# A tuned attention and expert kernel: the opening in two halves of two batches, x loaded chunk by chunk, input layouts by partition, value weights folded earlier

## The chip, the cores and the metric

The kernel runs on one core of one Trainium2 chip. The metric is the time of one execution on the device in microseconds (us). Three runs of the kernel before gave 667.72, 667.65 and 667.26 us, so the median is 667.65 us.

## The reference

x has 32 batches of 128 tokens of 128 features, the context 32 batches of 128 tokens of 64 features. Everything is f32.

```
x = x + tanh(g_xattn) * attention(layernorm(x), ctx)    # 16 heads of 64
        q = ln(x) @ Wq ; k = ctx @ Wk ; v = ctx @ Wv
        softmax(q k^T / 8) v, then @ Wo + bo
x = x + tanh(g_ffn) * experts(layernorm(x))             # 32 experts of 64, and a shared one of 128
        sigmoid router, 2 of 4 groups, then 8 experts; weights normalised, times 2.5
        sum over experts of w_e * down_e(silu(gate_e(x)) * up_e(x)), plus the shared expert
```

## The kernel before

The 32 batches are eight chunks of four. An attention stage runs over all chunks (chunk 0 unrolled, chunks 1 to 6 in a hardware loop, chunk 7 unrolled), then an expert stage over all chunks. Every engine has an instruction list of its own, written out by hand; the engines meet only in semaphores, and within an engine nothing overtakes. SyncE (SP) issues all DMAs, all of them in one queue.

Scores are not computed from q and k. A = Wq Wk^T is folded per head (`fold`, line 1255), and G = ln(x) A is projected per pair of batches (`g_project`, line 1161, into PSUM banks 0 to 3). Scores are then G times the context. In the same way C = Wv Wo replaces values and output projection. The block-diagonal tiles `wk_diag` and `wv_diag` are filled with zeros by GpSimd (POOL), lines 444 and 445, and SP loads the weights into them after that (`load_diag`, line 319). Products of f32 quality are made of three fp32r products of high and low parts: ScalarE (ACT) writes the high part (`xt_high`, `g_high`, `a_high`), VectorE (DVE) subtracts for the low part (`xt_low`, `g_low`, `a_low`).

For each batch t the row maxima are taken first: PE computes scores once (`max_scores`, line 1176), DVE reduces them (`take_max`, line 788), PE transposes the maxima (`transpose_max`, line 1193), ACT copies them out (`max_out`, line 540), and SP moves them by DMA into the tile `max_rows` (`load_max_row`, line 289), from where they enter the transposed scores (`scores`, line 1199) as a product with minus one. ACT takes the exponential, PE weighs the context (`weigh`, line 1219), and ACT copies the result out (`u_out`). The row sums go by DMA to another layout (`spread_sums`, line 297), DVE inverts them (`invert`, line 796), the inverse goes out to DRAM and back (lines 304 to 317), and DVE normalises (line 802).

The opening (the prologue) is what stands ahead of the loop on each engine:

- SP loads x of chunk 0, Wq, Wk, a context tile, Wv, Wo, small inputs, more context tiles, then x of chunks 1 to 7 in one DMA (line 344), two slices of the expert weights (`w_raw`), and then waits to send the row maxima of batch 0 (line 348).
- PE runs five products to keep itself busy (`keep_busy`), folds A in two halves, transposes ln(x) of four batches, projects G of batches 0 and 1 and of 2 and 3, takes the first scores of batches 0 and 1, and folds C last (lines 1282 to 1285).
- DVE computes the layer norm of chunk 0 (stats, 12 levels of small operations for the inverse root, and `apply` on four batches), then the low parts, then maxima of batch 0, the low parts of the second G, maxima of batch 1, and the stats of chunk 1 (`chunk_stats`, line 698).
- ACT writes the high parts, and computes tanh of the gates (line 584) once they and the bias have come in.

In chunk 0 of attention SP's order for batch b is: row maxima of b+1, sums of b-1, context and expert weights to come, inverse of b-1. On DVE chunk 0 holds extra work that later chunks don't have: the stats of chunks 2 to 7 (`STATS_AT`, line 70: chunks 2, 3, 4, 5 at steps 2, 3, 4, 5 and chunks 6 and 7 at step 6, where a step is half a batch), and the inverse roots for them. `invert` of the batch before stands ahead of the stats in the second half of a batch, and the low parts of the next G stand behind both.

```
            if h == 1:                                   # DVE, batch b, second half
                invert(t - 1, ...)
            ...
                chunk_stats(n)                           # first chunk only
            if h == 1 and b % 2 == 1 and not last:
                g_low(...)                               # scores of batch t + 1 wait for this
```

Of the kernel before, what the change touches and what calls it, by code (L numbers as in the profile page):

```python
# [31 lines left out]
P = 128  # L32
NB = 32
# [36 lines left out]
STATS_AT = {2: (2,), 3: (3,), 4: (4,), 5: (5,), 6: (6, 7)}  # L70
NB_SEAM = (NCH - 2) * CB
# [5 lines left out]
def build(nc, x, ctx_nat, ctx_t, g_xattn, g_ffn, wq_t, wk_t, wv_t, wo, bo, router_t, router_bias, experts, out):  # L77
    with ExitStack() as stack:
# [97 lines left out]
        fold_ps = (bank[0], bank[2])  # L176
        early_ps = ((bank[6:8], bank[4:6]), (bank[0:2], bank[4:6]))
# [3 lines left out]
        x_in = [sem("x_in0"), sem("x_in1")]  # L181
# [13 lines left out]
        xt_done, xhi_ready, xlo_ready = sem("xt_done"), sem("xhi_ready"), sem("xlo_ready")  # L195
        g_done, ghi_ready, glo_ready = sem("g_done"), sem("ghi_ready"), sem("glo_ready")
# [31 lines left out]
        x_dram = x.rearrange("b n d -> n b d")  # L228
        out_dram = out.rearrange("b n d -> n b d")
# [43 lines left out]
        def _(sp):  # L273
# [70 lines left out]
            sp.dma_start(x_sb[:, CB:NB, :], x_dram[:, CB:NB, :]).then_inc(x_in[1], 16)  # L344
            for slot in range(2):
                load_weights(slot, slot * WSTEP)
            sp.wait_ge(const_ready, 1)
            load_max_row(0, 0, -2)

            def attention(c, first, last):  # L350
                for b in range(CB):
                    t = CB * c + b
                    if not (last and b == CB - 1):
                        load_max_row(t + 1, (b + 1) % 2, t - 1)
                    if not (first and b == 0):
                        spread_sums(t - 1, (b - 1) % 2)
# [47 lines left out]
            def store_result(c):  # L404

                wait_first(result_ready, c + 1)
                sp.dma_start(out_dram[:, bass.ds(c * CB, CB), :], result.rearrange("p (b d) -> p b d", b=CB))\
                    .then_inc(result_free, 16)
# [34 lines left out]
        def _(pool):  # L443
# [64 lines left out]
            pool.wait_ge(x_in[1], 16)  # L508
# [16 lines left out]
        def _(act):  # L525
            def xt_high(i):
# [3 lines left out]
                nc.scalar.activation(xnt_hi[:], ut_ps[:], ACT.Copy).then_inc(xhi_ready, 1)  # L530

# [49 lines left out]
            xt_high(0)  # L581
            a_high(1)
            act.wait_ge(small_in, 16 * 3)
# [3 lines left out]
            g_high(0, 0)  # L587
# [101 lines left out]
        def _(dve):  # L689
# [8 lines left out]
            def chunk_stats(n):  # L698

                for b in range(CB):  # L700
                    nc.vector.bn_stats(bn6[:, 0, b, :], tile_of(CB * n + b)).then_inc(ln_step[0], 1)
                wait_first(ln_step[0], 2 * CB * n + CB)
                for b in range(CB):
                    nc.vector.bn_aggr(mean_var[:, 0, CB * n + b, :], bn6[:, 0, b, :]).then_inc(ln_step[0], 1)
                dve.wait_ge(ln_step[0], 2 * CB * (n + 1))

# [50 lines left out]
            def apply(which, t):  # L757

                for b in range(CB):
# [16 lines left out]
            def xt_low(i):  # L776
                dve.wait_ge(xhi_ready, i + 1)
                nc.vector.tensor_tensor(xnt_lo[:], ut_ps[:], raw(xnt_hi[:]), ALU.subtract).then_inc(xlo_ready, 1)

# [189 lines left out]
            dve.wait_ge(x_in[0], 16)  # L969
# [3 lines left out]
            ln_apply(0, 0)  # L973
# [8 lines left out]
            xt_low(0)  # L982
            a_low(1)
            g_low(0, 0)
# [3 lines left out]
            g_low(1, 1)  # L988
            for h in range(2):
# [3 lines left out]
            dve.wait_ge(x_in[1], 16)  # L993
            dve.wait_ge(const_ready, 6)
            chunk_stats(1)
# [151 lines left out]
        def _(pe):  # L1147
# [13 lines left out]
            def g_project(ring, chunk, bank_free):  # L1161

                pe.wait_ge(xlo_ready, chunk + 1)
                for j in range(4):
                    s, value = bank_free[j // 2]
                    wait(pe, s, value + j % 2)
# [281 lines left out]
```

## Time and profile before

| | |
|---|---|
| median of three runs | 667.65 us |
| profiled execution, its own time | 665.77 us |
| span of its trace | 664.0 us |
| PE busy | 650.2 us, 98% |
| DVE busy | 499.3 us, 75% |
| ACT busy | 365.4 us, 55% |
| POOL busy | 284.2 us, 43% |
| DMA queue q1 (all of SP's transfers) | 65.07 MB, 39.9% of 16 engines |
| TensorE clock granted | 1.00 of full |

PE is TensorE's matmul, PEld its weight load, SPq the issue of a DMA on SP. A number in brackets in a timeline is idle time of the engine ahead of the instruction, with what ended it. "issue" in the chain of waits is time in which the engine waited for nothing that the profile shows. A landing time is counted from the start of the issue to the data's arrival.

### The profile page before, as it was taken

Reading aid. Unit: us, or ns where it says so; the run is one execution under the profiler, and the core shown is the slowest. Engines: PE = TensorE matmul, PEld = TensorE weight load, DVE = VectorE, ACT = ScalarE, POOL = GpSimd, SP = SyncE. Lnnn points to the kernel's source line nnn. Section 1 sums busy time; section 2 is a strip of 40 time slices with the busy share of each in tenths; the row PEclk is TensorE's granted clock in tenths of the full one; section 3 lists DMA queues with packets and bytes.
Section 4 is the critical chain, followed back from the end, with each engine's and each line's share of the span. In section 5 each row is a group of like instructions: output and inputs, shape, how many; then the busy total and the mean of one; then the engine's idle time right before and its main releaser. Section 6 shows DMA issues by size and latency. Waiting matters only on the chain.

```text
span 664.0 us, 13629 instructions
## 1 busy us (share of the span) xinstructions
PE 650.2 (98%) x3668; PEld 472.1 (71%) x3668; DVE 499.3 (75%) x1331; ACT 365.4 (55%) x690; POOL 284.2 (43%) x316
## 2 busy tenths in 40 slices
PE   8999999999999999999999999999999999999997
PEld 5656666666667676676658778788887878888785
DVE  6989857777586775867787979968696877869565
ACT  3564556565465654655556455565655555555553
POOL 4222323233131332324202656656565656656553
PEclk9999999999999999999999999999999999999999
DMA  7323323232322323223225735273644536364650
GB/s 186 98 64 82 92 65 79 62 84 63 83 75 68 90 63 80 64 78 94 52 67 138 174 89 131 74 182 85 156 119 111 130 72 156 85 159 112 133 141 16
DMA packets 63276, 65.58 MB, mean 99 GB/s; under 512 B 26112, under 2 KB 41600, under 8 KB 63232
## 3 DMA queue, kind: packets, MB, share of 16 engines
q1 hardware_dynamic: 63232, 65.07, 39.9%
q8 instruction: 18, 0.29, 0.2%
q14 instruction: 26, 0.21, 0.1%
HBM read 61.64 MB, written 2.88 MB: 97 GB/s over the span
## 4 chain that ended last, share of the span: by engine, by line
PE 68%; issue 8%; POOL 8%; DVE 6%; DMA 5%; SPq 3%; ACT 1%; POOLq 0%; DVEq 0%; ACTq 0%
PE bank L1151 12%; PE bank L1227 12%; PE bank L1152 11%; PE bank L1153 11%; POOL halves L516 7%; PE bank L1251 6%; PE bank L1187 4%; PE bank L1207 2%; PE bank L1216 2%; PE bank L1210 2%; PE bank L1213 2%; DVE area L806 2%; DMA inverse_dram<-inverse 1%; DMA inverse_bc<-inverse_dram 1%; SPq L294 1%
## 5 line engine op out<-in xcount | busy, mean ns | idle before, releaser
L516 POOL TENSOR_TENSOR halves<-area,halves 128x512 fp32r<-128x512 f32 x134 | 174.0, 1299 | 141.0 <-ACT halves L650 136.5
L663 ACT ACTIVATE area<-bank 128x512 f32<-128x512 f32 x136 | 81.4, 598 | 109.3 <-PE bank L1153 106.7
L602 ACT ACTIVATE area<-bank 128x512 f32<-128x512 f32 x128 | 69.5, 595 | 117.3 <-PE bank L1216 117.3
L1107 DVE TENSOR_TENSOR bank<-area,bank 128x512 f32<-128x512 f32 x128 | 88.6, 692 | 51.1 <-PE bank L1153 50.8
L1227 PE MATMUL bank<-area,ctx_keys 128*65 128x512 f32 (+1 forms) x256 | 124.6, 599 | 0.2 <-ACT u_odd L550 0.2
L1151 PE MATMUL bank<-x2t_hi,w_hi 128*128 128x512 f32 x272 | 110.3, 405 | 1.4 <-DVE area L1118 1.3
L1152 PE MATMUL bank<-x2t_hi,w_lo 128*128 128x512 f32 x272 | 107.1, 394 | 0.0
L1153 PE MATMUL bank<-x2t_lo,w_hi 128*128 128x512 f32 x272 | 106.3, 391 | 0.0
L462 POOL TENSOR_TENSOR ctx_hi<-ctx_raw,ones_col 128x128 fp32r<-128x128 f32 x32 | 18.8, 588 | 197.3 <-DMA ctx_raw<-ctx_t 197.3
L792 DVE TENSOR_REDUCE row_max<-bank 128x4 f32<-128x512 f32 x128 | 81.7, 680 | 25.4 <-PE bank L1187 21.0
L650 ACT ACTIVATE halves<-area 128x512 fp32r<-128x512 f32 x136 | 85.1, 626 | 21.1 <-DVE area L1118 20.7
L1118 DVE TENSOR_TENSOR area<-bank,wbc 128x512 f32<-128x512 f32 x128 | 86.3, 679 | 1.5 <-DMA wbc<-rows_dram 1.5
L806 DVE TENSOR_TENSOR area<-u_odd,inverse_bc 64x1024 f32<-64x1024 f32 x32 | 39.9, 1248 | 42.7 <-DMA inverse_bc<-inverse_dram 42.2
L1251 PEld LDWEIGHTS bank<-c_pair,area 128*128 128x128 f32 x512 | 61.3, 192 | 11.2 <-issue 8.6
L1227 PEld LDWEIGHTS bank<-area,ctx_keys 128*65 128x65 f32 (+1 forms) x256 | 37.1, 164 | 39.3 <-issue 38.6
L1251 PE MATMUL bank<-c_pair,area 128*128 128x128 f32 x512 | 62.5, 275 | 0.0
L1151 PEld LDWEIGHTS bank<-x2t_hi,w_hi 128*128 128x128 f32 x272 | 51.1, 188 | 14.2 <-DVE area L1118 3.9
L1153 PEld LDWEIGHTS bank<-x2t_lo,w_hi 128*128 128x128 f32 x272 | 51.1, 188 | 12.0
L1152 PEld LDWEIGHTS bank<-x2t_hi,w_lo 128*128 128x128 f32 x272 | 51.2, 188 | 10.2
L1151 PE MATMUL bank<-halves,w_hi 128*128 128x512 f32 x136 | 54.3, 399 | 0.5 <-POOL halves L516 0.5
L1187 PEld LDWEIGHTS bank<-ctx_hi,halves 64*128 64x128 f32 x512 | 33.4, 186 | 30.1 <-issue 23.9
L1153 PE MATMUL bank<-halves,w_hi 128*128 128x512 f32 x136 | 53.9, 396 | 0.0
(129 smaller groups left out, 1087.7 us busy)
## 6 DMA issues: line engine op xcount, KB each, us to landing
wbc<-rows_dram SPq DMA_DIRECT2D x126, 256.0 KB, 4.4
inverse_bc<-inverse_dram SPq DMA_DIRECT2D x64, 256.0 KB, 3.9
w_raw<-experts SPq DMA_DIRECT2D x32, 102.0 KB, 2.0
ctx_raw<-ctx_t SPq DMA_DIRECT2D x32, 64.0 KB, 1.9
ctx_keys<-ctx_nat SPq DMA_DIRECT2D x32, 64.0 KB, 2.1
out<-area SPq DMA_DIRECT2D x7, 256.0 KB, 4.1
max_rows<-max_t SPq DMA_DIRECT2D x64, 4.0 KB
area<-wq_t SPq DMA_DIRECT2D x1, 512.0 KB, 4.4
```

Of the source, the lines that this page charges most:

```text
L516: nc.gpsimd.tensor_tensor(hid_lo[:, u % SLOTS, :], hid[:, u % HIDS, :], raw(hid_hi[:, u % SLOTS, :]), ALU.subtract).then_inc(hidlo_ready, 1)
L602: nc.scalar.activation(probs_t[:, k, :, :], st_ps[q][:].rearrange("p (h n) -> p h n", h=4), ACT.Exp)\
L650: nc.scalar.activation(hid_hi[:, u % SLOTS, :], hid[:, u % HIDS, :], ACT.Copy).then_inc(hidhi_ready, 1)
L663: nc.scalar.activation(silu_g[:, u % 2, :], gate_ps[u % 2][:], ACT.Silu).then_inc(silu_ready, 1)
L792: nc.vector.tensor_reduce(row_max[:, parity, first:first + 4], ps[q][:].rearrange("p (h m) -> p h m", h=4), AX_X, ALU.max)\
L1107: nc.vector.tensor_tensor(up_ps[u % UPS][:], silu_g[:, u % 2, :], up_ps[u % UPS][:], ALU.mult)\
L1118: nc.vector.tensor_tensor(hid[:, u % HIDS, :], up_ps[u % UPS][:], wbc[:, group % WBC_SLOTS, i, :], ALU.mult).then_inc(hid_ready, 1)
L1151: nc.tensor.matmul(ps, wh, xh, start=start, stop=False)
L1152: nc.tensor.matmul(ps, wl, xh, start=False, stop=False)
L1153: return nc.tensor.matmul(ps, wh, xl, start=False, stop=stop)
L1227: nc.tensor.matmul(u_ps[q][0:CD + 1 if q == 0 else P, :], keys, probs_t[:, k, :, :].rearrange("p i n -> p (i n)"), start=True, stop=True). ...
L1251: ins = nc.tensor.matmul(ps, u_t[:, parity, p, :], c_pair[:, p, :], start=p == 0, stop=p == PAIRS - 1)
```

## The change

- x, Wq, Wo and the output are laid out by partition: one partition's part of a transfer is one contiguous piece (2 KB for a chunk of x, 4 KB for Wq and Wo), where it was pieces of 512 B. The transposes of inputs and output are outside the kernel.
- x is loaded chunk by chunk: chunk 1 where chunks 1 to 7 stood, then the row maxima of batch 0, then the two slices of expert weights and chunk 2. Chunks 3 and 4 are issued in batch 0, chunks 5 and 6 in batch 1, chunk 7 in batch 2, each time behind the row maxima and ahead of the sums.
- Wk is loaded as soon as its own tile is zeroed.
- In the opening the norm's `apply`, the transposes and the high and low parts of ln(x) go in two halves of two batches. G of batches 0 and 1 needs the first half alone.
- On ACT tanh of the gates moves behind the high parts of the first G.
- C is folded ahead of the first scores of batch 1, where it was behind them.
- DVE takes the first step of chunk 1's stats ahead of the maxima of batch 1.

```diff
+X_AT = {0: (3, 4), 1: (5, 6), 2: (7,)}
+        xt_ps = bank[6:8]
-        x_in = [sem("x_in0"), sem("x_in1")]
+        x_in = [sem(f"x_in{n}") for n in range(NCH)]
 # SP
-            sp.dma_start(x_sb[:, 0:CB, :], x_dram[:, 0:CB, :]).then_inc(x_in[0], 16)
-            sp.dma_start(wq_pair, wq_t.rearrange("(p r) n -> r p n", r=P)).then_inc(wqk_in, 16)
-            sp.wait_ge(zeroed, 2)
+            def load_x(n):
+                tiles = slice(CB * n, CB * n + CB)
+                sp.dma_start(x_sb[:, tiles, :], x[:, tiles, :]).then_inc(x_in[n], 16)
+            load_x(0)
+            sp.dma_start(wq_pair, wq_t).then_inc(wqk_in, 16)
+            sp.wait_ge(zeroed, 1)
             for q in range(2):
                 load_diag(wk_diag, wk_t, q, wqk_in)
             load_raw(0, 0)
+            sp.wait_ge(zeroed, 2)
             for q in range(2):
                 load_diag(wv_diag, wv_t, q, wvo_in)
-            sp.dma_start(wo_pair, wo.rearrange("(p r) n -> r p n", r=P)).then_inc(wvo_in, 16)
+            sp.dma_start(wo_pair, wo).then_inc(wvo_in, 16)
...
-            sp.dma_start(x_sb[:, CB:NB, :], x_dram[:, CB:NB, :]).then_inc(x_in[1], 16)
+            load_x(1)
+            sp.wait_ge(const_ready, 1)
+            load_max_row(0, 0, -2)
             for slot in range(2):
                 load_weights(slot, slot * WSTEP)
-            sp.wait_ge(const_ready, 1)
-            load_max_row(0, 0, -2)
+            load_x(2)
 
             def attention(c, first, last):
                 for b in range(CB):
                     t = CB * c + b
                     if not (last and b == CB - 1):
                         load_max_row(t + 1, (b + 1) % 2, t - 1)
+                    if first:
+                        for n in X_AT.get(b, ()):
+                            load_x(n)
                     if not (first and b == 0):
                         spread_sums(t - 1, (b - 1) % 2)
...
-                sp.dma_start(out_dram[:, b:b + CB // 2, :],
+                sp.dma_start(out[:, b:b + CB // 2, :],
 # POOL
-            pool.wait_ge(x_in[1], 16)
 # ACT
+            def xt_high_half(half):
+                act.wait_ge((xt_begun, xt_done)[half], 1)
+                nc.scalar.activation(xnt_hi[:, halved(half)], xt_ps[half][:, halved(half)], ACT.Copy)\
+                    .then_inc((xhi_begun, xhi_ready)[half], 1)
             a_high(0)
-            xt_high(0)
+            xt_high_half(0)
             a_high(1)
+            g_high(0, 0, range(2))
+            xt_high_half(1)
+            g_high(0, 0, range(2, 4))
             act.wait_ge(small_in, 16 * 3)
             nc.scalar.activation(tanh_g[:], gates[:], ACT.Tanh).then_inc(tanh_ready, 1)
...
-            g_high(0, 0)
             g_high(1, 1, range(3))
 # DVE (chunk_stats is cut in chunk_stats_begin, which waits for x_in[n], and chunk_stats_end)
-            ln_apply(0, 0)
+            dve.wait_ge(rstd_step[0], RSTD_STEPS)
+            apply(0, 0, range(2))
             a_low(0)
-            xt_low(0)
+            xt_low_half(0)
+            apply(0, 0, range(2, 4))
             a_low(1)
-            g_low(0, 0)
+            g_low(0, 0, range(2))
+            xt_low_half(1)
+            g_low(0, 0, range(2, 4))
             (maxima of batch 0)
             g_low(1, 1)
+            chunk_stats_begin(1)
             (maxima of batch 1)
             dve.wait_ge(router_in, 32)
-            dve.wait_ge(x_in[1], 16)
             dve.wait_ge(const_ready, 6)
-            chunk_stats(1)
+            chunk_stats_end(1)
 # PE
             fold(wq_pair, wk_diag, 0, fold_ps[0])
             pe.wait_ge(const_ready, 6)
-            transpose_norm(0, ut_ps)
+            transpose_half(0)
             fold(wq_pair, wk_diag, 1, fold_ps[1])
-            g_project(0, 0, ((glo_ready, -2), (glo_ready, -2)))
+            g_project(0, 0, None, range(2))
+            transpose_half(1)
+            g_project(0, 0, None, range(2, 4))
+            pe.wait_ge(xlo_ready, 1)
             max_scores(0, 0, 0, 0, early_ps[0][0])
             max_scores(0, 0, 0, 1, early_ps[0][1])
             g_project(1, 0, ((glo_ready, 1), (glo_ready, 3)))
             transpose_max(0, 0)
+            pe.wait_ge(wvo_in, 16 * 3)
+            fold(wv_diag, wo_pair, 0, early_ps[0][0][0])
             pe.wait_ge(maxt_ready, 1)
+            fold(wv_diag, wo_pair, 1, early_ps[0][0][1])
             pe.wait_ge(glo_ready, 4 + 2)
             max_scores(1, 1, 0, 0, early_ps[1][0])
             max_scores(1, 1, 0, 1, early_ps[1][1])
-            pe.wait_ge(wvo_in, 16 * 3)
-            pe.wait_ge(max_ready, 2)
-            for i in range(2):
-                fold(wv_diag, wo_pair, i, early_ps[0][0][i])
```

## Rows read from the trace of the kernel before

**Rows 1.** The page: busy times, and PE's granted clock in 40 slices.
```profile
PE 650.2 (98%) x3668; PEld 472.1 (71%) x3668; DVE 499.3 (75%) x1331; ACT 365.4 (55%) x690; POOL 284.2 (43%) x316
...
PEclk9999999999999999999999999999999999999999
```

**Rows 2.** The chain of waits, 18 to 26 us: start us, us, what.
```profile
19.19 0.41 issue
...
25.28 0.83 issue
```

**Rows 3.** The chain of waits, 40 to 61 us.
```profile
40.41 0.28 issue
...
42.97 0.14 ACT max_t L543
...
45.39 1.85 DMA sums<-u_odd
...
60.82 0.50 PE bank L1207 x2
```

**Rows 4.** PE and weight loads in time order, opening: start us, us [idle before].
```profile
6.58 0.19 PEld L1264 LDWEIGHTS bank<-c_pair 128*128 128x128 f32 x1 [0.24 <-issue]
7.26 1.04 PEld L1258 LDWEIGHTS bank<-area 128*128 128x128 f32 x8 [0.49 <-DMA area<-wk_t]
...
11.28 0.38 PE L1151 MATMUL bank<-xnt_hi,a_hi 128*128 128x256 f32 x1 [0.52 <-DVE xnt_lo L778]
...
19.60 1.11 PE L1187 MATMUL bank<-ctx_hi,halves 64*128 64x128 f32 x16 [0.72 <-ACT max_t L543]
```

**Rows 5.** ACT in time order, opening.
```profile
12.27 0.20 ACT L584 ACTIVATE tanh_g<-gates 128x2 f32<-128x2 f32 x1 [0.88 <-DMA bo_bc<-bo]
```

**Rows 6.** DVE in time order, opening and first chunk.
```profile
10.53 0.69 DVE L778 TENSOR_TENSOR xnt_lo<-bank,xnt_hi 128x512 fp32r<-128x512 f32 x1 [0.68 <-ACT xnt_hi L530]
...
13.43 2.48 DVE L783 TENSOR_TENSOR halves<-bank,halves 128x512 fp32r<-128x512 f32 x4 [1.31 <-ACT halves L536]
...
20.61 2.47 DVE L792 TENSOR_REDUCE row_max<-bank 128x4 f32<-128x512 f32 x4
23.00 0.86 DVE L701 BATCH_NORM_STATS2 bn<-x_sb 128x6 f32<-128x128 f32 x4
24.02 0.38 DVE L704 BATCH_NORM_AGGREGATE mean_var<-bn 128x2 f32<-128x6 f32 x4 [0.15 <-DVE bn L701]
24.72 1.29 DVE L792 TENSOR_REDUCE row_max<-bank 128x4 f32<-128x512 f32 x2 [0.33 <-DVE mean_var L704]
...
36.56 0.25 DVE L800 RECIPROCAL inverse<-sums 128x16 f32<-128x16 f32 x1 [0.34 <-DMA sums<-area]
...
38.10 2.48 DVE L783 TENSOR_TENSOR halves<-bank,halves 128x512 fp32r<-128x512 f32 x4
```

**Rows 7.** SP's issues in time order.
```profile
27.61 0.38 SPq L280 DMA_DIRECT2D ctx_keys<-ctx_nat  x1
32.61 1.33 SPq L294 DMA_DIRECT2D max_rows<-max_t  x2
34.06 1.20 SPq L302 DMA_DIRECT2D sums<-area  x2
```

**Rows 8.** One line's instructions: SP's issue time in ns, min/median/max.
```profile
L287 SPq DMA_DIRECT2D w_raw<-experts x6: 351/356/4572, 13.2 to 55.3; - x6
L407 SPq DMA_DIRECT2D out<-area x7: 524/524/1510, 414.2 to 639.1; - x7
```

**Rows 9.** DMA issues of the page: count, KB each, median us to landing.
```profile
out<-area SPq DMA_DIRECT2D x7, 256.0 KB, 4.1
...
x_sb<-x SPq DMA_DIRECT2D x1, 256.0 KB, 2.9
...
out<-area SPq DMA_DIRECT2D x2, 128.0 KB, 1.9
...
gates<-g_xattn SPq DMA_DIRECT2D x1, 0.5 KB, 4.1
```

More of the change, by code:

```diff
@@ L225, in wait @@
             eng.wait_ge(s, value)
-        x_dram = x.rearrange("b n d -> n b d")
-        out_dram = out.rearrange("b n d -> n b d")
         def pairs_of(h):
@@ L406, in store_result @@
                 wait_first(result_ready, c + 1)
-                sp.dma_start(out_dram[:, bass.ds(c * CB, CB), :], result.rearrange("p (b d) -> p b d", b=CB))\
+                sp.dma_start(out[:, bass.ds(c * CB, CB), :], result.rearrange("p (b d) -> p b d", b=CB))\
                     .then_inc(result_free, 16)
@@ L705, in chunk_stats @@
                 dve.wait_ge(ln_step[0], 2 * CB * (n + 1))
+            def chunk_stats(n):
+                chunk_stats_begin(n)
+                chunk_stats_end(n)
             def batch_stats(t, b):
@@ L755, in rstd_level, with apply @@
                     ins.then_inc(stepped, 1)
-            def apply(which, t):
-                for b in range(CB):
+            def apply(which, t, batches=range(CB)):
+                for b in batches:
                     nc.vector.tensor_scalar(xn[:, b, :], tile_of(t + b),
@@ L778, in xt_low, with xt_low_half @@
                 nc.vector.tensor_tensor(xnt_lo[:], ut_ps[:], raw(xnt_hi[:]), ALU.subtract).then_inc(xlo_ready, 1)
+            def xt_low_half(half):
+                dve.wait_ge((xhi_begun, xhi_ready)[half], 1)
+                nc.vector.tensor_tensor(xnt_lo[:, halved(half)], xt_ps[half][:, halved(half)], raw(xnt_hi[:, halved(half)]),
+                                        ALU.subtract).then_inc((xlo_begun, xlo_ready)[half], 1)
             def g_low(g, ring, banks=range(4)):
@@ L1159, in transpose_norm, with transpose_half, g_project @@
                 ins.then_inc(xt_done, 1)
[L1161 to L1166, printed above, removed]
+            def transpose_half(half):
+                pe.wait_ge(xn_ready, 2 * half + 2)
+                for i in range(2 * half, 2 * half + 2):
+                    ins = nc.tensor.transpose(xt_ps[half][:, i * P:(i + 1) * P], xn[:, i, :], ident[:])
+                ins.then_inc((xt_begun, xt_done)[half], 1)
+            def g_project(ring, chunk, bank_free, banks=range(4)):
+                if bank_free is None:
+                    pe.wait_ge(xlo_begun, 1)
+                else:
+                    pe.wait_ge(xlo_ready, chunk + 1)
+                for j in banks:
+                    if bank_free is not None:
+                        s, value = bank_free[j // 2]
+                        wait(pe, s, value + j % 2)
                     if j % 2 == 0:
@@ L1423, with by_pair @@
     ctx = np.asarray(ctx_512)
+    def by_pair(w):
+        return lay(np.asarray(w).reshape(PAIRS, P, D).transpose(1, 0, 2))
     def up(w, shared):
@@ L1443 @@
     ins = [nc.dram_tensor(n, a.shape, F32, kind="ExternalInput").ap() for n, a in arrays.items()]
-    out = nc.dram_tensor("out", (NB, P, D), F32, kind="ExternalOutput").ap()
+    out = nc.dram_tensor("out", (P, NB, D), F32, kind="ExternalOutput").ap()
     build(nc, *ins, out)
     r = run_bass_kernel_spmd(nc, [arrays], core_ids=[0])
-    return r.results[0]["out"]
+    return lay(np.asarray(r.results[0]["out"]).transpose(1, 0, 2))
```

12 lines of the change are left out of this document (7 added, 5 removed).

## The prediction

> **What bounds the kernel now.** I read the page first: PE is busy for 650.2 of 664.0 us at full granted clock [rows 1]. So a change in the opening can give back no more than PE's own gaps there, and whatever moves the first chunk moves everything behind it, one for one, as long as PE stays the engine that the rest waits for. The chain of waits comes next, since it shows where PE is not the bound. In the opening it leaves PE twice: 0.41 us at 19.2 and 0.83 us at 25.3 [rows 2]. PE's own timeline has the first of these as 0.72 us of idle time ahead of the first scores of batch 1, ended by ACT's copy of the maxima [rows 4]. From 26.1 to 40.4 PE has no idle time. Then comes a third stretch [rows 3], and it is the one that decides this case: PE waits 0.28 us at 40.41, the chain goes over ACT's `max_out` (42.97) to SP, which issues the maxima and then the sums of batch 1, the sums land at 47.24 after 1.85 us, DVE inverts them at once, and from there DVE's list of chunk 0 (normalise, stats, maxima, low parts) ends just ahead of PE's scores at 60.82. So between 40 and 61 us the end is set by an SP queue, a small DMA and a full DVE, not by PE. DVE's own timeline shows the same thing one batch earlier: the inverse of batch 0 at 36.56 was preceded by 0.34 us of waiting for the sums, and behind it stand the stats and the four `g_low` from 38.10 to 40.58, which end just ahead of PE's scores at 40.69 [rows 6].
>
> **The opening, step by step.** PE's fold of A begins at 7.26, after 0.49 us in which its weight load waited for Wk [rows 4]. The weight load before it had a gap of 0.24 us, which is the warm-up's own pace, so 0.25 us can go at most when Wk comes sooner (SP waits for one memset instead of two). I take 0.25; bounds 0 and 0.25. Then the halves. Before, DVE needs `apply` on four batches, then the low part of A, and waits 0.68 us for ACT's high part, and `xt_low` takes 0.69; PE starts G at 11.28 [rows 4 to 6]. Now `apply` on two batches is ready at about 8.3, PE transposes two batches at 8.3 to 8.6, ACT writes the high part of A 8.3 to 8.9 and half of x 8.9 to 9.25 (half of the 0.68), DVE does `a_low` to 9.65 and half of `xt_low` (0.35) to 10.0. G starts at 10.05, 1.2 us sooner. ACT is no longer held by tanh, which waited for a DMA until 12.27 [rows 5]; high parts of G start at about 11.1. With six products a bank at 0.12 us, the two transposes between, and one high and one low part of about 0.6 us each behind bank 3, the four `g_low` end at 14.8 where they ended at 15.91 (13.43 + 2.48) [rows 6]: 1.1 us sooner.
>
> From there DVE is full in both versions: four maxima (2.47), four `g_low` (2.48), and now one `bn_stats` group (0.86) ahead of the maxima of batch 1 instead of behind them. That puts these maxima at 20.65 to 23.15 where they ended at 23.08, and the first scores of batch 2 on PE must wait for them. PE has meanwhile folded C in the gap of 0.72 us, but it gains nothing by it: it ends the scores of batch 0's first half near 22.6 and waits for DVE at 23.2. The `bn_aggr` (0.38) and the start-up of 0.33 seen ahead of 24.72 [rows 6] bring the maxima of batch 2 to 23.95, against 24.72. **Gain of the opening: 0.77 us**, bounds 0.4 (if the half-size instructions cost what whole ones do: about 0.35 more in all) and 1.66 (both gaps, 0.72 + 0.83, and 0.1 of change, if DVE turned out not to hold PE). I take 0.77 since it is the sum of DVE's rows.
>
> **The x loads inside batches 0 to 2.** Chunks 3 and 4 go behind the maxima of batch 1, where SP has time: it issues nothing from 28.0 to 32.6 [rows 7], so their cost is nothing; without that gap it would be two issues. Chunks 5 and 6 are otherwise. SP is held until ACT copies out the maxima of batch 2 (issue at 32.61, now 31.84 with the 0.77), issues them for 1.33 us, and then directly the sums at 34.06 [rows 7]. Two loads now stand between. No row of before issues such a load in a quiet queue; the nearest are 0.35 us (102 KB) and 0.52 us (256 KB, out) [rows 8]. I take 0.45 and 0.05 between two issues, so 1.0 us, bounds 0.8 and 1.15. The sums are issued 1.0 - 0.77 = 0.23 us later than before. The second load is in the queue as well: a load of 256 KB takes 2.9 us to land [rows 9], the second sum DMA is issued 1.15 us after it and needs 1.85, so the load lands at the very time the sums would; I add 0.1. The inverse of batch 0, which waited for these sums even before, comes 0.3 us later than 36.56, and with it `g_low`, and with that PE's scores at 40.69: **the whole gain of the opening is gone, and 0.3 us more** (bounds -0.3 and +0.75). The cost of SP's two issues is paid whole because what DVE has saved is spent waiting.
>
> Chunk 7 goes behind the maxima of batch 3, again directly ahead of the sums, and this is the chain of [rows 3] itself: SP's maxima, sums, 1.85 us, DVE. Nothing hides it. **0.45 + 0.05 = +0.5 us** (bounds 0.4 and 0.57). Its data are through the rings before the sums' (1.1 us between their issues, as above). DVE is full from there to 60.7, so it carries to PE at 60.82. PE had 0.82 us of slack ahead of `g_low` at 59.8, so it takes no part.
>
> **What stays.** The stats of chunks 2 to 7 find their x in time: chunk 7 is issued near 45 and lands near 48, its stats are at 52. Chunk 1's stats no longer wait (x lands at about 15). The one transfer of chunks 1 to 7 blocked SP's issue of `w_raw` for up to 4.57 us [rows 8], but SP then waited for ACT's maxima anyway, so that gain is 0. The end: two stores of 128 KB land in 1.9 us after issue [rows 9], which is also what 4 KB of sums take, so their bytes cost hardly anything; 0 to 0.1 for larger pieces, I take 0.05.
>
> The Trainium skill's page "DMA: Bandwidth & Descriptors" (Specifications) has 512 B as the smallest piece for full rate. By that rule the new layout gives nothing, as pieces were 512 B already; if instead the first x and Wk landed 0.3 us sooner, the fold would still wait for the warm-up, so the sum is the same but for the 0.25 above. No row of before holds a load of 2 KB pieces of x.
>
> **The sum.** +0.3 + 0.5 - 0.05 = +0.75 us. The profiled execution took 665.77 us around a span of 664.0, the median is 1.88 us above the former: I predict 666.5 for such an execution with a span of 664.7, and 667.65 + 0.75 = **668.4 us** for the median. That is 0.11%: a measurement of this kernel tells about 0.2% (1.3 us) from no change, so the forecast is "no change", a shade slower.
>
> **Rivals.**
>
> A. *The loads are hidden, the opening's gain survives.* If SP issued the x loads in idle time, or the sums were not late, -0.77 - 0.05: 666.8 us. For it: 0.34 us of waiting at 36.56 is short [rows 6], and an issue may be cheaper than I take. Against: SP's order puts the loads between two DMAs that follow one another directly [rows 7]. Chance 0.23.
>
> B. *Slower: the sums queue behind x.* Place: the same two points. From 3.0 us on for the landing of chunk 6 (1.15 + 1.85) each further tenth is added to the inverse. A 0.5 KB DMA of the gates, issued behind 512 KB of Wo, took 4.1 us to land [rows 9]. If x5 and x6 land like the 256 KB stores (4.1 us), the sums of batch 0 are 37.9 against 36.5, +1.35, and chunk 7 adds 48.85 - 47.24 = +1.6: 670.6 us; half of it gives 669.5. Against: the first x took 2.9. Chance 0.17. The same page, in "Queues, rings and completion order", says that each DMA engine consumes its ring in order and that a semaphore's increment lands only after all earlier writes of that engine; by this rule B's queueing is real, and only the bytes ahead decide its size. The trace agrees in the gates' 4.1 us.
>
> C. *Faster by more than the bound.* Both gaps of PE vanish (0.72 + 0.83 and 0.1, as above), and neither load costs anything: -1.65, 666.0 us. For it: PE's list has the work to fill the first gap. Against: DVE is full from 13.4 to 24.4 [rows 6], and PE can't pass it. Chance 0.18, more than the rows give, since a gain in one of the many small moves may be missing in my sum.
>
> **How the numbers follow.** The forecast (between +0.1 and +1.3) has 0.42, A with all between -1.3 and +0.1 has 0.23, B 0.17, C 0.18. C and most of B lie beyond 0.2%. Faster 0.18, same 0.65, slower 0.17. The range leaves out half of C and the far part of B: 666.2 to 669.6 us. The forecast's own bounds are -0.3 + 0.4 - 0.1 = 0.0 and 0.75 + 0.57 = +1.3: 667.65 to 669.0.
>
> **What would show it.** In the changed kernel's trace: G starts near 10.05; the maxima of batch 1 end near 23.2 and PE waits for them with 0.5 us or more; the first maxima of batch 2 near 23.95; SP issues chunk 5 near 33.2 and the sums near 34.3; DVE's inverse of batch 0 near 36.9 with over 1 us of waiting for sums; PE's scores of batch 2 near 41.0 with about 1 us of idle ahead; the inverse of batch 1 near 48.05; PE's scores of batch 4 near 61.6 (60.82 + 0.8). If these scores come ahead of 60.8, the step that fails is the price of SP's issues; if they are right and the time is not, something behind 61 us has moved, which I hold to be carried over unchanged.

## The result, and the profile after

The changed kernel is slower. On the first chip it took 670.15 us (median of 8, 668.93 to 671.58) against 667.92 us for the kernel before (8 runs): ratio 1.0036, interval 1.0025 to 1.0048, or about +2.4 us (the medians differ by 2.2). A second chip gave 667.58 against 665.13 us (12 and 24 runs), ratio 1.0034, interval 1.0023 to 1.0044. The prediction was 668.4 us, or +0.75 us, "no change", with a range of 666.2 to 669.6. The profiled execution took 671.03 us around a span of 669.2. That is 5.2 us over the one of before, more than the medians differ, so below each reading is set against a second profile of each kernel.

The start first. TensorE's weight loads in the changed kernel (columns: start us, us, engine, line and operation; in brackets the idle time before and what ended it):

```profile
5.90 0.34 PEld L1310 LDWEIGHTS bank<-c_pair 128*128 128x128 f32 x1 [0.52 <-issue]
7.33 0.19 PEld L1310 LDWEIGHTS bank<-c_pair 128*128 128x128 f32 x1 [0.24 <-issue]
8.19 0.19 PEld L1304 LDWEIGHTS bank<-area 128*128 128x128 f32 x1 [0.24 <-DMA area<-wk_t]
```

In the warm-up a load takes 0.34 us until 7.3 us and 0.19 from there: the step from half to full speed, though the column of the granted clock says 1.00 throughout. The fold of A starts at 8.19, where it started at 7.26 [rows 4]. Wk is issued sooner than before (1.72 us against 2.61), but it is not there sooner: it lands at 8.02 here, against 7.22 in the kernel before.

The opening behind it, in VectorE's and TensorE's timelines:

```profile
20.79 0.86 DVE L719 BATCH_NORM_STATS2 bn<-x_sb 128x6 f32<-128x128 f32 x4
21.64 2.48 DVE L824 TENSOR_REDUCE row_max<-bank 128x4 f32<-128x512 f32 x4
25.10 1.29 DVE L824 TENSOR_REDUCE row_max<-bank 128x4 f32<-128x512 f32 x2 [0.69 <-DVE mean_var L725]
24.38 0.66 PE L1233 MATMUL bank<-ctx_hi,halves 64*128 64x128 f32 x8 [0.75 <-DVE row_max L824]
```

VectorE runs full and TensorE waits for its maxima (0.75 us), as forecast. From the first weight load of the fold to the maxima of batch 2 it is 16.91 us (25.10 - 8.19), against 17.46 (24.72 - 7.26) in [rows 4, 6].

SyncE's queue around the sums of batch 0 and of batch 1, against [rows 7]:

```profile
32.99 1.34 SPq L295 DMA_DIRECT2D max_rows<-max_t  x2
34.37 0.91 SPq L326 DMA_DIRECT2D x_sb<-x  x2
35.40 1.20 SPq L303 DMA_DIRECT2D sums<-area  x2
45.20 1.41 SPq L295 DMA_DIRECT2D max_rows<-max_t  x2
46.65 0.43 SPq L326 DMA_DIRECT2D x_sb<-x  x1
47.20 1.19 SPq L303 DMA_DIRECT2D sums<-u_odd  x2
```

And the inverses and scores that wait for those sums, against [rows 3, 6]:

```profile
38.49 0.25 DVE L832 RECIPROCAL inverse<-sums 128x16 f32<-128x16 f32 x1 [1.33 <-DMA sums<-area]
50.06 0.25 DVE L832 RECIPROCAL inverse<-sums 128x16 f32<-128x16 f32 x1 [1.24 <-DMA sums<-u_odd]
42.61 0.50 PE L1253 MATMUL bank<-halves,ctx_hi 64*128 64x512 f32 x2 [0.54 <-issue]
63.57 0.50 PE L1253 MATMUL bank<-halves,ctx_hi 64*128 64x512 f32 x2 [0.32 <-DVE halves L815]
```

The sums of batch 0 are issued 2.41 us behind the beginning of the maxima's issue (before 1.45), and VectorE idles 1.33 us for them (before 0.34). The scores of batch 4 are 2.75 us late. Behind that the distance still grows, by different amounts: this profile is 4.9 us behind that of before at the last inverse, and the two second profiles, 2.06 us apart at S4 below, are 3.0 us apart there. No run isolates this part.

Three marks cut the start into pieces that can be compared over all twelve profiles. F is the fold's first weight load, I0 and I1 are the inverses of batch 0 and 1, S4 the first scores of batch 4, in us from the span's start:

| profile | F | I0 - F | I1 - I0 | S4 |
|---|---|---|---|---|
| before | 7.26 | 29.30 | 10.70 | 60.82 |
| before, second | 7.46 | 29.12 | 10.70 | 60.99 |
| E4 layouts alone | 7.60 | 29.09 | 10.70 | 60.90 |
| changed | 8.19 | 30.30 | 11.57 | 63.57 |
| changed, second | 7.79 | 30.23 | 11.51 | 63.05 |
| E9 x5, x6 in one DMA | 7.79 | 29.63 | 11.56 | 62.49 |
| E5 three small issues | 8.19 | 30.34 | 11.25 | 63.29 |
| E1 x all in batch 0 | 8.47 | 28.73 | 11.07 | 61.78 |
| E8 x behind the sums | 7.81 | 28.59 | 11.39 | 61.30 |
| E6 stats 1 in batch 0 | 7.78 | 30.09 | 11.38 | 62.96 |
| E7 warm-up 4 | 7.44 | 29.75 | 11.09 | 61.79 |
| E10 stats 1 in the gap | 7.44 | 28.55 | 11.06 | 60.55 |

The changed kernel loses in each column: 0.3 to 0.9 us at F, 1.0 to 1.1 in I0 - F, 0.8 to 0.9 in I1 - I0. F is not a perfect mark. Where Wk sets it (E8 and E9), the maxima of batch 2 are issued 24.5 us behind it; where the warm-up sets it (both profiles of the changed kernel, E1, E5) it is 24.8. So differences of 0.3 us in I0 - F between these two kinds say nothing.

For the landing one more table is needed. Each row is the second of a pair of sums DMAs, with what was issued directly ahead of the pair; times in us from the span's start.

| profile, batch | directly ahead | it lands at | sums issued | sums land |
|---|---|---|---|---|
| before, batch 0 | nothing | - | 34.66 | 36.54 |
| E1, batch 0 | nothing | - | 35.31 | 37.17 |
| changed, batch 0 | x5, x6 | 38.11 | 36.00 | 38.47 |
| changed, second, batch 0 | x5, x6 | 37.65 | 35.59 | 37.99 |
| E9, batch 0 | x5 and x6 in one | 36.99 | 34.79 | 37.40 |
| E5, batch 0 | two of 0.5 KB | 38.15 | 35.99 | 38.50 |
| changed, batch 1 | x7 | 49.70 | 47.78 | 50.04 |
| E5, batch 1 | one of 0.5 KB | 49.32 | 47.85 | 49.76 |

With nothing ahead the sums land 1.86 to 1.88 us after their issue. With a DMA ahead they land 0.34 to 0.44 us behind it, unless their own 1.86 us end later: in the last row 47.85 + 1.86 is 49.71, so there the DMA ahead costs next to nothing. In these rows the sums are never complete before what stood ahead of them, and the price is set by when that lands.

### The profile page after: what moved, and what is told of

It is laid out like the page before. It is cut to its first block, busy times and chain, and to the rows that moved or that the text cites. A ratio compares the mean times of both kernels' runs of the same rounds, so it can differ in the third digit from the quotient of the medians.

```text
span 669.2 us, 13635 instructions
## 1 busy us (share of the span) xinstructions
PE 652.6 (98%) x3668; PEld 472.5 (71%) x3668; DVE 500.8 (75%) x1332; ACT 365.7 (55%) x691; POOL 286.0 (43%) x316
## 3 DMA queue, kind: packets, MB, share of 16 engines
HBM read 61.64 MB, written 2.88 MB: 96 GB/s over the span
## 4 chain that ended last, share of the span: by engine, by line
PE 53%; issue 11%; DMA 9%; POOL 8%; DVE 7%; SPq 6%; ACT 2%; DVEq 1%; POOLq 0%; ACTq 0%
PE bank L1186 11%; PE bank L1187 10%; PE bank L1188 10%; POOL halves L525 7%; PE bank L1273 7%; DMA inverse_bc<-inverse_dram 4%; PE bank L1297 3%; PE bank L1233 3%; SPq L295 2%; DMA inverse_dram<-inverse 2%; DVE area L838 2%; PE bank L1253 2%; DVE halves L815 2%; DVE row_max L824 2%; DMA sums<-area 1%
## 5 line engine op out<-in xcount | busy, mean ns | idle before, releaser
L472 POOL TENSOR_TENSOR ctx_hi<-ctx_raw,ones_col 128x128 fp32r<-128x128 f32 x32 | 21.4, 667 | 199.3 <-DMA ctx_raw<-ctx_t 199.3
```

## The experiments

Ratios are to the kernel before on the same chip, with their intervals. E2 and E3 are each half of the change. Line numbers are those of each kernel's own file.

**E1, all remaining x in batch 0.**

```
-X_AT = {0: (3, 4), 1: (5, 6), 2: (7,)}
+X_AT = {0: (3, 4, 5, 6, 7)}
```

> The changed kernel with x chunks 3 to 7 all issued in batch 0, where SP has about 4 us of idle time, and none in batches 1 and 2. Theory 1 (SP's issues of x and the x data ahead of the sums are what costs): in the changed kernel the sums of batch 0 left 0.96 us later behind the maxima and landed after 2.45 instead of 1.85 us, those of batch 1 0.47 us later and after 2.26 instead of 1.85 us; all four go, -2.4 us against the changed kernel, so the time is within 0.2% of before (667.0 to 668.8 us), the sums follow the maxima by 1.45 to 1.55 us, and PE's scores of batch 4 start near 61.2. Theory 2 (the loss comes from the opening and from waits in later chunks, the loads are nearly free): at most -0.8 us, so 669.3 or more.

Measured: 666.40 against 666.26 us, 1.0001 (0.9991 to 1.0011). The five loads are issued in 2.34 us that SyncE has free (E1's queue and VectorE's inverses):

```profile
27.35 2.34 SPq L326 DMA_DIRECT2D x_sb<-x  x5
34.70 1.20 SPq L303 DMA_DIRECT2D sums<-area  x2
37.20 0.25 DVE L832 RECIPROCAL inverse<-sums 128x16 f32<-128x16 f32 x1 [0.33 <-DMA sums<-area]
48.27 0.25 DVE L832 RECIPROCAL inverse<-sums 128x16 f32<-128x16 f32 x1 [0.74 <-DMA sums<-u_odd]
```

The wait for the sums of batch 0 is back at 0.33 us, the loss is gone. The place of three loads is the whole slowdown, as far as an interval of 0.1% to either side can tell; all else together is worth nothing that can be measured.

In batch 1 VectorE still waits 0.74 us (before 0.38), though nothing stands directly ahead of the sums. Their landing is told in 16 steps; 15 have come by 47.93 us and the last at 48.25. While these packets move, from 47.10 to 47.45, one transfer of 8 KB runs in an instruction queue (E1's DMA from 47.0 to 47.5: queue, kind, packets, MB, share of 16 engines):

```profile
q14 instruction: 1, 0.01, 4.3%
```

E2, E6, E7, E8 and E10 have the same late last step, by 0.3 to 0.7 us, each with such a transfer among or just ahead of the packets; the kernel before and E4 have neither. This coincidence was not tested by a run.

**E8, the same loads in the same batches, behind the sums.**

```
+                    if not (first and b == 0):
+                        spread_sums(t - 1, (b - 1) % 2)
                     if first:
                         for n in X_AT.get(b, ()):
                             load_x(n)
-                    if not (first and b == 0):
-                        spread_sums(t - 1, (b - 1) % 2)
```

> The changed kernel with one move: SP issues the sums first and the x loads behind them, in the same batches (x3, x4 in batch 0; x5, x6 in 1; x7 in 2). Same loads, same bytes, same SP time in all. Theory 1 (the cost is that a load stands ahead of the sums, on the path SP, sums, inverse): sums 1.45 us behind the beginning of max_rows in batch 1 and not 2.4, inverse of batch 0 within 0.4 us of the wait-free value, time that of the kernel with all x in batch 0: ratio 1.000 to 1.001 to the kernel before. Theory 2 (any x load near the sums costs, before or behind, since it delays ctx, w_raw and the inverses behind it in the queue): ratio 1.002 to 1.0035, with the idle time at inverse_dram or inverse_bc instead.

Measured: 667.79 against 667.21 us, 1.0010 (0.9999 to 1.0021). In E8's queue:

```profile
33.74 1.20 SPq L303 DMA_DIRECT2D sums<-area  x2
34.98 1.05 SPq L326 DMA_DIRECT2D x_sb<-x  x2
```

and on its VectorE:

```profile
36.40 0.24 DVE L832 RECIPROCAL inverse<-sums 128x16 f32<-128x16 f32 x1
46.24 1.22 DVE L838 TENSOR_TENSOR area<-area,inverse_bc 64x1024 f32<-64x1024 f32 x1 [0.43 <-DMA inverse_bc<-inverse_dram]
```

The sums no longer make VectorE wait at all in batch 0. Theory 1 holds for most of the loss. A part of theory 2 is there as well: the inverse's broadcast is now what comes late (0.43 us, where the changed kernel, E1 and the kernel before have no wait).

**E5, three DMAs of 0.5 KB in place of x5, x6 and x7, on top of E1.**

```
+for n in {1: (0, 1), 2: (2,)}.get(b, ()):
+    sp.dma_start(tiny[:, n:n + 1], g_xattn...broadcast_to([P, 1])).then_inc(tiny_in, 16)
```

> The kernel with all five remaining chunks of x loaded in batch 0 (ratio 1.0001 to the kernel before), plus three DMAs of 0.5 KB that nothing waits for, issued by SP where the changed kernel issues x5, x6 and x7: two between max_rows and sums of batch 1, one between them in batch 2. It has the changed kernel's time on SP's queue, and none of its 256 KB in the rings. Theory 1 (SP's issue time is most of the +2.4 us): sums is issued 2.4 us after max_rows begins in batch 1 (instead of 1.45) and 0.45 later in batch 2, lands in 1.85 us as before, the inverse of batch 0 is 0.9 to 1.0 later than in that kernel and the time +1.4 us, ratio about 1.002. Theory 2 (the transfers of x ahead of sums are the cost): the time is that kernel's, ratio 0.999 to 1.001. Estimate from the changed kernel's trace (0.96 and 0.47 us of issue, 0.6 and 0.4 of landing): +1.4 of the 2.4 stays.

Measured: 668.78 us, 1.0056 (1.0034 to 1.0078), beside 1.0034 for the changed kernel on that chip. E5's queue and inverse:

```profile
34.35 0.91 SPq L368 DMA_DIRECT2D tiny<-g_xattn  x2
35.38 1.21 SPq L305 DMA_DIRECT2D sums<-area  x2
38.53 0.25 DVE L837 RECIPROCAL inverse<-sums 128x16 f32<-128x16 f32 x1 [1.93 <-DMA sums<-area]
```

Theory 1 had the issue right and the landing wrong, and theory 2 fails. 1 KB ahead of the sums costs in I0 - F what 512 KB do (30.34 against 30.30 us): the same 0.91 us of issue, and a landing of the sums of batch 0 in 2.5 us, where the changed kernel has 2.4 to 2.5 and E1, E8 and the kernel before, with nothing directly ahead, have 1.8 to 1.9. The reason is in the table: the second of the small DMAs lands 3.3 us after its issue, as late as x6 (3.3 us). So bytes alone do not set the price. What does is not separated here: each small DMA writes 4 bytes to each of 128 partitions, so it has as many pieces as a load of x, and no run had a DMA of few pieces in this place. E5's higher median has another part: in half of its runs the granted clock is 0.997, and in its profile the expert stage falls back by a further 1.3 us between 400 and 655 us, which no row of the first 64 us explains.

**E9, x5 and x6 as one DMA of 512 KB.**

```
-X_AT = {0: (3, 4), 1: (5, 6), 2: (7,)}
+X_AT = {0: (3, 4), 2: (7,)}
+if b == 1:
+    sp.dma_start(x_sb[:, CB * 5:CB * 7, :], x[:, CB * 5:CB * 7, :]).then_inc(x_pair, 16)
```

> The changed kernel with chunks 5 and 6 of x in one DMA of 512 KB instead of two of 256 KB, in the same place ahead of the sums of batch 1. Theory 1 (what costs is the number of issues, their time on SP and one more DMA in the rings ahead of the sums, and not the bytes): sums issued 0.45 us sooner than in the changed kernel, landing 2.1 us instead of 2.45, time 0.5 to 0.8 us below the changed kernel: ratio 1.002 to 1.003 to before. Theory 2 (bytes in the rings): issue 0.45 us sooner, but the sums land as much later, ratio 1.0034 as for the changed kernel.

Measured: 669.57 us, 1.0041 (1.0028 to 1.0055), 5 runs. In E9:

```profile
33.63 0.44 SPq L365 DMA_DIRECT2D x_sb<-x  x1
34.18 1.20 SPq L304 DMA_DIRECT2D sums<-area  x2
37.42 0.25 DVE L835 RECIPROCAL inverse<-sums 128x16 f32<-128x16 f32 x1 [1.24 <-DMA sums<-area]
```

From the issue of the maxima to the inverse it is 5.17 us, against 5.50 and 5.44 in the changed kernel: one issue less (0.48 us) brings 0.3. The rest goes in the landing, 2.6 and 2.9 us for the two sums DMAs, not shorter, so half of each theory holds. (Of the 0.6 us that I0 - F is shorter, the other 0.3 stands ahead of the queue, from the mark F.) One DMA ahead thus delays the landing no less than two, which a price per DMA would not give. The time does not follow: its interval overlaps the changed kernel's. For the time this run is inconclusive.

**The changed kernel again.**

> The changed kernel again, on the chip of the three others, for a comparison without a change of chip and a second profile. Expected: ratio 1.003 to 1.005; sums 2.4 us behind the beginning of max_rows in batch 1, landing 2.3 to 2.6 us; scores of batch 2 1.3 to 1.9 us later than in the kernel before and of batch 4 2.2 to 2.8. If the landing of sums were 1.85 us here, the rings would not be part of the cause.

Measured: ratio 1.0034, S4 at 63.05, sums issued 2.41 us behind the maxima, landing in 2.4 us in batch 0 and 2.2 in batch 1: as expected.

**The kernel before again.**

> The kernel before again, for a second profile. If the time at which TensorE's clock rises in the warm-up (4.8 us in the first profile, 6.5 to 7.6 in those of the new opening) varies from execution to execution, the fold starts here at 7.3 to 8.6 us; if it belongs to the kernel's order, at 7.3 again. Sums land in 1.85 us in both batches if that is the price without other DMAs ahead.

Measured: 665.98 us, profiled once. Its weight loads:

```profile
5.04 0.34 PEld L1264 LDWEIGHTS bank<-c_pair 128*128 128x128 f32 x1 [0.52 <-issue]
5.74 0.19 PEld L1264 LDWEIGHTS bank<-c_pair 128*128 128x128 f32 x1 [0.37 <-issue]
7.46 0.19 PEld L1258 LDWEIGHTS bank<-area 128*128 128x128 f32 x1 [0.24 <-DMA area<-wk_t]
```

The clock rose at 5.7 us here and at 4.8 in the first profile, with the same instructions on TensorE. Over all profiles the rise lies between 4.8 and 7.6 us, so it varies by execution. Where it is early, Wk sets F (E8 and E9: Wk lands at 7.8 us); where it is late, the warm-up does.

**E7, four warm-up products instead of five, on top of E1** (`-WARM_UP, GAP = 5, 1` / `+WARM_UP, GAP = 4, 1`).

> The kernel with all remaining x in batch 0, and four warm-up matmul groups instead of five. Theory 1 (the fold's start is set by the warm-up, run in the trace at half speed until 7.3 to 8.0 us, and by Wk only if that lands later): fold starts up to 0.86 us sooner, time -0.3 to -0.8 us, ratio 0.9988 to 0.9995. Theory 2 (Wk's landing, at about 7.3 to 7.6 us, sets it): no change, ratio 1.000. Theory 3 (with less warm-up the clock is still low when the fold begins): the fold's own weight loads take 0.34 us instead of 0.19 and the opening is up to 1 us longer, ratio 1.0005 to 1.0015.

Measured: 666.05 us, 1.0014 (0.9999 to 1.0029). F is 7.44 with Wk the last to come, a microsecond sooner than in E1, and then it is lost (E7 by stretch: us, busy time of the engines, granted clock, DMA share, GB/s):

```profile
20.00:24.00 4.00, 2.87 (x34) 2.26 (x32) 3.54 (x12) 1.77 (x3) 1.24 (x3) 1.00 0.41 122
24.00:28.00 4.00, 4.00 (x23) 2.27 (x20) 3.31 (x13) 0.27 (x1) 0.32 (x1) 0.57 0.16 46
```

TensorE was busy for 2.87 of 4 us, and then its granted clock fell to 0.57 as the mean of 4 us, so to the lower level, 1.2 GHz, for most of them. Four other profiles have 2.86 to 2.88 us in the same stretch without a fall (the second of the changed kernel, E6, E8, E9), and only 4 of E7's 12 runs show 0.997 or less over the span. So the fall explains this profile, not the median: the other eight runs have a median of 665.96 us. None of the three theories had this.

**E6, the statistics of chunk 1 moved to batch 0, on top of E1.**

```
-STATS_AT = {2: (2,), 3: (3,), 4: (4,), 5: (5,), 6: (6, 7)}
+STATS_AT = {0: (1,), 2: (2,), 3: (3,), 4: (4,), 5: (5,), 6: (6, 7)}
-            chunk_stats_begin(1)
-            chunk_stats_end(1)
```

> The kernel with all remaining x in batch 0, and the statistics of chunk 1 moved from ahead of the maxima of batch 1 to batch 0 behind the first row of maxima of batch 2. Theory 1 (in the opening VectorE is the engine that runs full from the maxima of batch 1, and what stands on it ahead of the maxima of batch 2 delays them one for one): the 0.86 + 0.38 us of bn_stats and bn_aggr leave, of which 0.5 to 0.9 is gained at the scores that wait for row_max, ratio 0.9985 to 0.999 to the kernel before. Theory 2 (that time is given back behind: the same VectorE work then stands ahead of the inverse of batch 0, and TensorE, which waits for sums, starts batch 2 no sooner): ratio 1.000 to 1.0005.

Measured: 668.79 us, 1.0049 (1.0031 to 1.0067), worse than either theory. E6's VectorE:

```profile
21.23 2.48 DVE L824 TENSOR_REDUCE row_max<-bank 128x4 f32<-128x512 f32 x4 [0.77 <-PE bank L1231]
24.80 1.29 DVE L824 TENSOR_REDUCE row_max<-bank 128x4 f32<-128x512 f32 x2 [1.09 <-PE bank L1231]
```

The room is not used: TensorE folds C (1.95 us) ahead of the scores of batch 1, so VectorE waits for it, and behind it the later maxima and the inverse slip (I0 - F 30.09 against 28.73). So in the opening two engines hold the end at once. The time has a second part, below.

**E10, chunk 1's statistics in VectorE's gap, C folded later.** `load_x(1)` stands right behind Wk, `chunk_stats(1)` right behind the first `apply`, and on TensorE:

```
-            fold(wv_diag, wo_pair, 0, early_ps[0][0][0])
-            pe.wait_ge(maxt_ready, 1)
-            fold(wv_diag, wo_pair, 1, early_ps[0][0][1])
             max_scores(1, 1, 0, 0, early_ps[1][0])
             max_scores(1, 1, 0, 1, early_ps[1][1])
+            fold(wv_diag, wo_pair, 0, early_ps[0][0][0])
+            pe.wait_ge(maxt_ready, 1)
+            fold(wv_diag, wo_pair, 1, early_ps[0][0][1])
```

> A version meant to beat both: the kernel with all remaining x in batch 0, chunk 1 of x loaded right behind Wk, its statistics (0.86 + 0.38 us of VectorE) done in the 1.73 us in which VectorE waits for the high part of A, and the fold of C behind the first scores of batch 1 again, since in the kernel with these statistics in batch 0 TensorE's fold held VectorE's maxima of batch 1 for 0.77 us. Theory 1 (VectorE and the fold of C are together what sets the maxima of batch 2): maxima of batch 2 15.6 us behind the fold's start instead of 16.49, everything to the scores of batch 4 0.7 to 0.9 us sooner, ratio 0.9985 to 0.9992 to before. Theory 2 (the load of x ahead of the context delays the context or Wv, or the fold of C now holds TensorE): ratio 1.000 to 1.001. If TensorE idles more and its granted clock falls, the ratio is above 1.002.

Measured: 668.37 us, 1.0025 (1.0014 to 1.0037). It is the earliest of all at S4 (60.55 us) and yet slower than both E1 and the kernel before. At 410 us, in the first expert chunk, the same instruction of VectorE in E10:

```profile
408.59 0.70 DVE L1141 TENSOR_TENSOR bank<-area,bank 128x512 f32<-128x512 f32 x1 [0.39 <-issue]
410.00 1.23 DVE L776 TENSOR_TENSOR ln_small<-ln_small 128x8 f32<-128x8 f32 x1
414.50 0.51 PE L1185 MATMUL bank<-x2t_hi,w_hi 128*128 128x512 f32 x1 [0.81 <-DVE area L1152]
```

and in E1:

```profile
410.39 0.35 DVE L776 TENSOR_TENSOR ln_small<-ln_small 128x8 f32<-128x8 f32 x1
```

A stall of 0.39 and one of 0.9 us that have no releaser, and TensorE waits 0.81 us for it. E6 has the same two stalls on the same instructions, E1, the changed kernel and the kernel before have not. Against E1's profile everything behind moves by 1.25 us. E6 and E10 are the two kernels in which VectorE's instructions ahead of that point stand in another order than in the changed kernel. That the stall is the fetch of VectorE's code falling elsewhere is a guess, not shown: E1 too has an instruction transfer of 8 KB at this place (410.79 us, in E10 410.17) and no stall. Without the 1.25 us E10 would be at about 667.1 us (668.37 - 1.25), which is the kernel before, not a gain.

**E4, the layouts alone:** the kernel before, x still in two DMAs, with

```
-            sp.dma_start(wq_pair, wq_t.rearrange("(p r) n -> r p n", r=P)).then_inc(wqk_in, 16)
+            sp.dma_start(wq_pair, wq_t).then_inc(wqk_in, 16)
...
-            sp.dma_start(x_sb[:, CB:NB, :], x_dram[:, CB:NB, :]).then_inc(x_in[1], 16)
+            sp.dma_start(x_sb[:, CB:NB, :], x[:, CB:NB, :]).then_inc(x_in[1], 16)
```

and the same for `wo` and `out`.

> The kernel before with the new layouts of x, Wq, Wo and the output alone; two DMAs of x and SP's order as before. Theory 1: the pieces of 512 B were at full rate already, so the first x lands in 2.9 to 3.1 us, Wk no sooner than 7.2 us, and the time is within 0.2% of before. Theory 2 (larger pieces land faster): Wk lands by 0.3 us or more sooner, and the stores at the end too, 0.3 to 0.6 us faster. Theory 3 (larger pieces hold up what is behind them in the rings): the Wk DMAs land later than in before and the fold starts later, up to +0.5 us.

Measured: 665.71 against 666.26 us, 0.9992 (0.9982 to 1.0003), all marks as before. The layouts are free, and may give a few tenths.

**E2, the opening alone, with the old loads:** the changed kernel with its new loads undone, among them

```
-            load_x(1)
+            sp.dma_start(x_sb[:, CB:NB, :], x_dram[:, CB:NB, :]).then_inc(x_in[1], 16)
...
-                    if first:
-                        for n in X_AT.get(b, ()):
-                            load_x(n)
...
-                dve.wait_ge(x_in[n], 16)
+                dve.wait_ge(x_in[min(n, 1)], 16)
```

> The kernel before with the new order on PE, ACT and DVE in the opening (halves, tanh later, C folded sooner, first stats step sooner) and with SP's list, layouts and the one large load of x as before. Theory 1: the opening is worth what DVE's rows give, 0.77 us less the 0.25 for Wk, and nothing eats it: 0.5 us faster than before, 667.0 to 667.6. Theory 2: the opening's gain hangs on when the weight clock of PE rises and on Wk's landing, both outside this edit; with both as before G starts about 1 us sooner, and the time is 0.5 to 1.0 us less. Theory 3 (the new order itself loses, since PE now waits for DVE's maxima): same as before or up to +0.5 us.

Measured: 671.01 us, 1.0076 (1.0061 to 1.0092), slower than any of the three theories. In E2's VectorE and TensorE:

```profile
22.92 0.87 DVE L712 BATCH_NORM_STATS2 bn<-x_sb 128x6 f32<-128x128 f32 x4 [2.38 <-DMA x_sb<-x]
26.43 0.77 PE L1226 MATMUL bank<-ctx_hi,halves 64*128 64x128 f32 x8 [2.41 <-DVE row_max L817]
```

and by stretch:

```profile
24.00:28.00 4.00, 1.59 (x11) 1.12 (x11) 3.24 (x10) 1.35 (x3) 1.00 (x2) 0.86 0.00 2
28.00:32.00 4.00, 4.00 (x18) 2.01 (x16) 3.45 (x15) 0.00 (x0) 0.00 (x0) 0.50 0.24 61
```

The statistics ahead of the maxima of batch 1 wait 2.38 us for the one large x load, TensorE waits 2.41 us for the maxima, and then it runs at half speed (granted clock 0.50). The early place of these statistics needs the load by chunks.

**E3, all loads as in the changed kernel, with the old opening:** the kernel before with

```
-            sp.dma_start(x_sb[:, CB:NB, :], x_dram[:, CB:NB, :]).then_inc(x_in[1], 16)
+            load_x(1)
...
+                    if first:
+                        for n in X_AT.get(b, ()):
+                            load_x(n)
```

and the layouts of E4.

> The kernel before with all of the new loading (layouts, x by chunks, order of the first loads), and its opening on PE, ACT and DVE as it was. Theory 1: sums of batch 0 later by 0.96 + 0.6, of batch 1 by 0.47 + 0.4, together 2.4 us slower than before: 670.0 to 670.6 us, PE's scores of batch 4 near 63.2. Theory 2 (loads nearly free): within 0.8 us of before.

Measured: 673.61 us, 1.0111 (1.0093 to 1.0128), three times the loss of theory 1. In E3's queue and VectorE:

```profile
35.37 1.21 SPq L301 DMA_DIRECT2D sums<-area  x2
40.71 0.25 DVE L808 RECIPROCAL inverse<-sums 128x16 f32<-128x16 f32 x1 [3.83 <-DMA sums<-area]
```

and by stretch:

```profile
40.00:44.00 4.00, 0.89 (x6) 0.40 (x5) 3.11 (x12) 0.90 (x2) 2.41 (x5) 0.85 0.14 26
44.00:48.00 4.00, 3.92 (x19) 2.36 (x18) 3.18 (x12) 1.09 (x3) 0.00 (x0) 0.50 0.47 125
```

The sums are issued at the changed kernel's time and land after up to 4.7 us instead of 2.4; TensorE idles 3.1 us, and its clock falls to half. All four runs show a clock of 0.994 or 0.995.

The loads ahead are not what takes so long: 30 of the 32 steps of the sums' landing have come by 38.33 us, as in the changed kernel, and the last two come at 40.52 and 40.69. A transfer of 16 KB in an instruction queue lasts from 37.87 to 39.45 us (E3's DMA from 37.8 to 38.3):

```profile
q1 hardware_dynamic: 141, 0.06, 44.3%
q8 instruction: 1, 0.02, 19.7%
```

All packets of the sums but seven have moved by 37.85, and those seven move from 39.44 on, as that transfer ends. So the trace points to one of the 16 DMA engines that was held by it; in the changed kernel a transfer of that size comes at 43.4 us, well behind these sums. No run moved it to test this.

## Why the prediction was wrong

It had the path right (SyncE's issues ahead of the sums, on a chain that TensorE waits for) and mis-sized two terms of the sum.

**The price of x in the rings failed.** The issue time was right: 0.96 us for x5 and x6 (predicted 1.0) and 0.47 for x7 (0.5). The landing was not. "I add 0.1" stands against +0.5 to 0.6 us in batch 0, and "through the rings before the sums'" against +0.3 to 0.4 in batch 1. The prediction let x6 land after 2.9 us, at the very time of the sums, and let the sums land with it. The runs show 3.2 to 3.3 us for x6 and 3.0 for x7, and the sums 0.34 to 0.36 us behind. In E5 1 KB has the same price in batch 0, so reasoning about bytes could not find it. In batch 1 the 0.4 us are x7's in the changed kernel (with one small DMA there, E5 pays 0.05); E1 and E10 reach the same 2.23 us with nothing ahead by their late last step, which is another thing.

**The earlier Wk failed.** Predicted -0.25 us; F is later by 0.3 to 0.9. Wk lands at 7.1 to 8.0 us in the ten profiles that issue it 0.9 us sooner, and at 7.1 to 7.6 in the four that do not. The clock's rise, which the prediction did not treat as a variable, comes on top.

**The halves were about right.** Predicted 0.52 us without Wk's part; from F to the maxima of batch 2 they give 0.55 in the first profiles and 0.40 in the second, and 0.7 to 0.9 in E8 and E9, where Wk sets F as it does before. In E1, where nothing covers them, 0.4 to 0.6 us are left at I0.

**"The whole gain of the opening is gone" was right,** as was the place: VectorE waits for sums, 1.33 us (predicted over 1). Its size is I0 - F: +1.0 us, where the prediction's marks give +0.6 (36.9 - 7.01 = 29.89, against 29.30 before).

Together, on the second profiles of both kernels, which differ by 2.06 us at S4: the predicted 0.8 there, 0.58 at F (+0.33 for -0.25), and 0.4 each for the two landings, are 2.2 us. The medians differ by 2.2 to 2.5. The first profiles differ by 2.75 at S4, since there F alone is 0.93 later. Rival B ends on that side (+1.9 to +3.0), and names the sums behind x. Its mechanism, sums that queue behind x, is the one that the landings show (it was given 0.17). That bytes decide the size is what E5 refutes. The Trainium skill's page "DMA: Bandwidth & Descriptors", section "Queues, rings and completion order", says that a semaphore's increment lands only after every earlier write of that DMA engine; the landings, 0.34 to 0.44 us behind whatever stood ahead, agree with that, and the prediction's reading of it, "only the bytes ahead decide its size", was its own and wrong.

## What to carry to other kernels

When a small DMA sits on the path from one engine to the next, issue it first: here each issue ahead cost 0.47 us on the queue, even at 0.5 KB, and the small DMA then landed 0.34 to 0.44 us behind what stood ahead, wherever that was later than its own 1.86 us; what stood ahead took 2.6 to 3.3 us to land at 0.5 KB and 3.4 at 512 KB. Move bulk loads to where the queue has idle time of its own, and cost a moved load by issue and by landing. Compare openings from a mark behind the clock's rise, since it moves a start by up to a microsecond between executions.

## What the runs showed of the hardware that was not expected

- TensorE's warm-up reaches full speed at 4.8 to 7.6 us in executions with the same instructions until then, and the granted clock's column says 1.00 all the while; the weight load's 0.34 or 0.19 us tells it.
- Short idle stretches cost twice. A gap of 2.4 us (E2) or 3.1 us (E3) was followed by a granted clock of 0.50; in E7 a stretch with 2.87 of 4 us busy was followed by 0.57, in four others with 2.86 to 2.88 the clock stayed at 1.00.
- One late step out of 16 can hold a landing: in E3 by 2.4 us while a 16 KB instruction transfer ran, in E1 by 0.3 us next to one of 8 KB.
- A reordering at 10 us brought a stall of 1.25 us at 410 us, on one instruction that nothing released (E6, E10).
